# Graph attention kernel: TensorE's block numbers read as one load of ten bytes a group instead of two loads of five words

## The chip, the cores and the metric

The kernel runs on 1 core of one Trainium2 chip. The metric is the device time of one execution in microseconds (us), the median of several runs; lower is better. Engines are named as the profile names them: PE is TensorE (PEld its weight loads), DVE VectorE, ACT ScalarE, POOL GpSimd, SP SyncE. Each engine has a sequencer of its own, written PEq, DVEq and so on, which works through the engine's instruction stream: it waits on semaphores, computes addresses in registers, reads values from memory into registers, and hands matmuls and other work to the engine's queue.

## The reference, cut to what matters

Three graph attention layers over 3125 nodes and 50,000 edges that are sorted by destination, then a mixture of experts. The change lies in the sum over edges of the attention layers:

```
def _gat_layer(x, W, attn_l, attn_r, bias, src, dst, num_heads, head_dim, use_elu):
    z = (x @ W).reshape(N, num_heads, head_dim)
    el = jnp.sum(z * attn_l, axis=-1)
    er = jnp.sum(z * attn_r, axis=-1)
    e = jax.nn.leaky_relu(el[src] + er[dst], NEG_SLOPE)
    m = jax.ops.segment_max(e, dst, num_segments=N)
    ex = jnp.exp(e - m[dst])
    denom = jax.ops.segment_sum(ex, dst, num_segments=N)
    alpha = ex / denom[dst]
    out = jax.ops.segment_sum(alpha[:, :, None] * z[src], dst, num_segments=N)
    ...
x = _gat_layer(node_features, W0, al0, ar0, b0, src, dst, 12, 64, True)
x = _gat_layer(x, W1, al1, ar1, b1, src, dst, 12, 64, True)
x = _gat_layer(x, W2, al2, ar2, b2, src, dst, 1, 768, False)
```

## The kernel before

The program is a chain of stages: a setup, then for each layer `l` a **node sweep** (the product with W, tile by tile of 128 nodes, written to a table in HBM) and an **edge sweep**, then a layer norm with routing, and the experts. In the trace the three edge sweeps stand at 250 to 902, 1107 to 1760 and 1954 to 2608 us.

**An edge sweep** walks over 415 visits. A visit is a tile of 128 edges together with one of 25 blocks of 128 destination nodes. POOL gathers the 128 source rows of a visit by an indirect DMA (L672) into a ring of 20 places, DVE multiplies them by their weights (L1492), and PE adds them up: a one-hot matrix of the visit times the rows, 384 and 396 columns wide, into the accumulator of the visit's block (`add_up`, L1047). Which accumulator it is, and which part of `erp` (the destination side of the attention logits) a visit needs, depends on the block number b(k) of visit k, which is known only at run time. So PE's sequencer must have b(k) in a register before it can issue.

**Groups.** Five visits make a group (G = 5), 83 groups a sweep (NG). Four groups (jj = 0 to 3, NBUF = 4) make one trip of a loop on the device (`pe.Fori`, L1070 in the profile); the last trip, of three groups, stands outside of the loop. The places of a trip are numbered at = jj * 5 + j.

**What PE does for a group**, in the order in which it is written, in `body`: visits j = 0 to 4; behind visit 1 the `er_of_edges` products (three small matmuls of 24 columns each, L1022) of two visits of the group three ahead (ER_LEAD = 3), which is 6 matmuls, and behind visit 3 those of the other three visits, 9 matmuls. DVE and ACT make of them the weights of that group.

**Two forms of visit.** Most visits are two fp32 matmuls, of which the trace has four records (two passes each). The places in SPLIT (2, 7, 10, 12, 17 in the first two layers, 1, 4, 7, 11, 14, 17 in the third) are done as two fp32r parts, `parts`: also four records, but shorter ones. Ahead of either PE's sequencer waits on semaphores of DVE and ACT: for the rows, the one-hot matrix and a free accumulator.

**Block numbers.** The setup on DVE writes b(k) as int32 into `b_k`, and from there copies: `b_of` for PE (83 rows of five, in a pitch of 8 words, and three rows of zeros at the end), `b_g` for ACT (first block of a group and of the next), `turns` for POOL (in the experts). PE's sequencer reads a row of `b_of` by `blocks_of(g)` (L1012), one TENSOR_LOAD of five values with a register instruction (FUSED_REGOPS) for its address ahead of it. In a group there are two: `now`, the group's own row, ahead of visit 0, and `later`, the row of group g + 3, behind visit 0. Ahead of each sweep three more groups have only their `er_of_edges` (45 matmuls), each behind a load.

The edge loop of PE is the only code that the change moves:

```
now = blocks_of(g)
for j in range(G):
    add_up(g, i, jj, j, now[j])
    if j == 0 and ahead:
        later = blocks_of(g + ER_LEAD)
    if j in (1, 3) and ahead:
        for n in ((0, 1), (2, 3, 4))[j // 2]:
            er_of_edges(g + ER_LEAD, (jj + ER_LEAD) % NBUF, n, later[n])
```

Of the kernel before, what the change touches and what calls it, by code (L numbers as in the profile page):

```python
# [8 lines left out]
I32 = mybir.dt.int32  # L9
U32 = mybir.dt.uint32  # L10
U8 = mybir.dt.uint8
# [14 lines left out]
G = 5  # L26
NBUF = 4
IN_ARENA = 3
ER_LEAD = 3
# [3 lines left out]
NG = V // G  # L33
# [14 lines left out]
NS = (TOP * N + EX * (P - 1)) // P  # L48
# [8 lines left out]
class Chain:  # L57
# [5 lines left out]
    def link(self, instruction):  # L63

        self.mark(instruction)
        self.follow()
# [33 lines left out]
def gnn_ffn(nc, x, edges, gnn, ffn, out):  # L100
    with ExitStack() as ctx:
        def sb(name, shape, dt=F32):
            return ctx.enter_context(nc.sbuf_tensor(name, shape, dt))
# [62 lines left out]
        src_k = sb("src_k", [P, V], I32)  # L166
        dst_k = sb("dst_k", [P, V])
        b_k = sb("b_k", [1, V + 1], I32)
        b_g = sb("b_g", [1, NG, 4], I32)
        b_of = sb("b_of", [1, NG + ER_LEAD, 8], I32)  # L170
        ends = sb("ends", [1, NB], I32)
        turns = sb("turns", [1, NS], I32)
        erm = sb("erm", [P, NB, 2 * HMAX])
        ert = sb("ert", [P, NB, HMAX])
        erp = sb("erp", [P, NB * 3 * 2 * HMAX], BF16)
# [247 lines left out]
        def at_place(j, b):  # L423

            return place_first[:, j, b, :] if b < EARLY else place_last[:, j, b - EARLY, :]
# [5 lines left out]
        def numbers():  # L431

            at = 8 * D + TOP * NB * NS
            return arena_h[:, at:at + 2 * TOP * NB * NS].rearrange("p (w j b s) -> p w j b s", w=2, j=TOP, b=NB)
# [494 lines left out]
        def _(pe):  # L929
# [74 lines left out]
            def edge_sweep(l):  # L1004
# [2 lines left out]
                for bank in range(4):  # L1007
                    nc.tensor.matmul(PS[:, bank, :], zeros_h[:, 0:P], zeros_h[:, :], start=True, stop=True)

                def blocks_of(g):  # L1010

                    return nc.values_load_multi_w_load_instructions(  # L1012
                        b_of[0:1, bass.ds(g, 1), 0:G].rearrange("o i j -> o (i j)"), engines=[mybir.EngineType.PE],
                        min_val=0, max_val=NB - 1,
                        skip_runtime_bounds_check_because="b(k) is a sum of NB - 1 comparisons")[1]

                def er_of_edges(g, jj, j, b):

                    if j == 0:
                        pe.wait_ge(s_ST, g + (NG * l + 1))  # L1020
                    for part in range(3):
                        o = nc.tensor.matmul(er_of(l, jj)[:, j, :], ST_b[:, jj, j * P:(j + 1) * P],  # L1022
                                             erp[:, bass.ds(b * (6 * H) + part * 2 * H, 2 * H)],
                                             start=(part == 0), stop=(part == 2))
                    if j == G - 1:
                        o.then_inc(s_er, 1)
# [23 lines left out]

                def body(i, last):
                    groups = LAST_GROUPS if last else NBUF
                    for jj in range(groups):
                        g = NBUF * i + jj
                        ahead = not last or jj + ER_LEAD < groups
                        now = blocks_of(g)
                        for j in range(G):
                            add_up(g, i, jj, j, now[j])
                            if j == 0 and ahead:
                                later = blocks_of(g + ER_LEAD)  # L1060
                            if j in (1, 3) and ahead:
                                for n in ((0, 1), (2, 3, 4))[j // 2]:
                                    er_of_edges(g + ER_LEAD, (jj + ER_LEAD) % NBUF, n, later[n])

                pe.wait_ge(s_erm, l + 1)
                for g in range(ER_LEAD):
                    now = blocks_of(g)
                    for j in range(G):
                        er_of_edges(g, g, j, now[j])
                with pe.Fori(0, NI - 1) as i:  # L1070
                    body(i, False)
                body(NI - 1, True)

            for l in range(3):
                node_sweep(l)
                edge_sweep(l)
# [44 lines left out]
            for j in range(TOP):  # L1121
                pe.wait_ge(s_onehots, j + 1)
                pe.wait_ge(s_numbered, j + 1)
                for b in range(NB):
                    if b == EARLY:
                        pe.wait_ge(s_late_places, j + 1)
                    o = nc.tensor.matmul(PS[:, 6, 0:2 * NS], at_place(j, b), numbers()[:, :, j, b, :],
                                         start=(j == 0 and b == 0), stop=(j == TOP - 1 and b == NB - 1))
# [70 lines left out]
        def _(dve):  # L1199
            dc = Chain(dve, s_dve)  # L1200
            link = dc.link
# [54 lines left out]
            starts = b_k[0:1, 0:V].rearrange("o (g j) -> o g j", j=G)  # L1256
# [1 line left out]
            link(nc.vector.tensor_copy(b_g[0:1, :, 0:1], starts[:, :, 0:1]))  # L1258
            link(nc.vector.tensor_copy(b_g[0:1, 0:NG - 1, 1:2], starts[:, 1:NG, 0:1]))
            link(nc.vector.memset(b_of[0:1, :, :], 0))  # L1260
            link(nc.vector.tensor_copy(b_of[0:1, 0:NG, 0:G], starts))
            link(nc.vector.tensor_copy(ends[0:1, 0:NB - 1], enter[0:1, :]))
            link(nc.vector.memset(ends[0:1, NB - 1:NB], V))
            augment_first((2, 3, 4))
# [595 lines left out]
```

## Time and profile before

| | |
|---|---|
| median of 3 runs | 2812.51 us (2811.25 to 2815.1) |
| span of the profiled execution | 3059.8 us |
| mean granted TensorE clock in it | 0.964 |
| PE, PEld busy | 2691.3, 1838.6 us (88%, 60%) |
| DVE, ACT, POOL busy | 2096.8, 1244.9, 1506.0 us |
| chain that ended last | PE 50%, DVE 21%, issue 13% |

The profiled execution has its own time, the 3059.8 us of its span, which is 247 us (8.8%) more than the median of the runs that were timed. Durations below come from that one execution. PE is busy for most of it, but a busy PE isn't PE at its peak: the end of a matmul is modelled, and a record lasts longer than the time until the next one can start. So times between starts are read, rather than durations, where matmuls stand in a row. What the sequencer does (loads of registers, register arithmetic) counts as idle on the engine's line; it can be seen where one asks for a source line.

### The profile page before, as it was taken

The numbers are of one execution on the slowest core, as the hardware profiler recorded it, in microseconds if no ns is written. First come the engines' busy times: TensorE is split into PE (matmuls) and PEld (weight loads), VectorE is DVE, ScalarE is ACT, GpSimd is POOL, SyncE is SP. The second block draws the span as 40 slices with busy tenths as digits, with TensorE's granted clock in tenths as the row PEclk, the third lists the DMA queues.
The fourth block names the chain that finished last, engine by engine and source line by source line (L and its number), as shares of the span: only waits on it lengthen the run. The fifth ranks groups of instructions, "written<-read, shape, count | busy, mean of one in ns | idle before, by whom it ended". The sixth has DMA issues, their size and how long they took to land.

```text
span 3059.8 us, 57119 instructions
## 1 busy us (share of the span) xinstructions
PE 2691.3 (88%) x14056; PEld 1838.6 (60%) x14060; DVE 2096.8 (69%) x3895; ACT 1244.9 (41%) x2607; POOL 1506.0 (49%) x1528
## 2 busy tenths in 40 slices
PE   3997999998989979898989999788898889759998
PEld 2884555555558855555555578555555555547776
DVE  6776888888887768888878877545555555673332
ACT  1224555555544435555555544223222223622211
POOL 1005666666631156666666412466666665114443
PEclk9998999999999979999999999899999999979999
DMA  6447888888867878888888767788888887967776
GB/s 210 169 148 251 289 286 291 291 290 290 289 219 205 210 228 292 289 287 290 291 287 288 250 191 216 218 281 285 279 282 281 282 282 258 397 217 145 145 146 118
DMA packets 199261, 762.09 MB, mean 249 GB/s; under 512 B 41889, under 2 KB 58033, under 8 KB 198542
## 3 DMA queue, kind: packets, MB, share of 16 engines
q0 software_dynamic: 127632, 604.14, 64.8%
q1 hardware_dynamic: 53790, 108.21, 11.6%
q10 hardware_dynamic: 17760, 48.79, 4.0%
q8 instruction: 36, 0.59, 0.1%
q14 instruction: 43, 0.35, 0.0%
HBM read 640.01 MB, written 133.45 MB: 253 GB/s over the span
## 4 chain that ended last, share of the span: by engine, by line
PE 50%; DVE 21%; issue 13%; ACT 4%; DMA 4%; another core or an unknown queue 3%; SPq 2%; POOL 1%; DVEq 1%; ACTq 1%; POOLq 0%
PE PS L1047 30%; DVE arena L1492 5%; PE PS L1176 5%; PE PS L978 4%; PE PS L1165 4%; PE PS L980 2%; DVE parts L1509 2%; PE PS L1022 2%; DMA arena<-table,src_k 2%; SPq L493 1%; DVE ST_b L1445 1%; DVE arena L1357 1%; DVE arena L1367 1%; DVE arena L1335 1%
## 5 line engine op out<-in xcount | busy, mean ns | idle before, releaser
L672 POOL DMA_INDIRECT arena<-table,src_k x945 | 959.9, 1016 | 500.8 <-issue 213.1
L1047 PE MATMUL PS<-arena,S 128*128 128x384 f32 (+1 forms) x1848 | 706.8, 514 | 57.8 <-issue 46.3
L1492 DVE TENSOR_TENSOR arena<-arena,PS 128x768 f32<-128x768 f32 x630 | 575.2, 946 | 0.9 <-ACT arena L822 0.9
L1047 PEld LDWEIGHTS PS<-arena,S 128*128 128x128 f32 x1848 | 335.5, 194 | 282.7 <-issue 156.8
L1047 PE MATMUL PS<-parts,S 128*128 128x384 f32 (+2 forms) x1332 | 340.4, 375 | 57.2 <-issue 51.0
L672 POOL DMA_INDIRECT W<-table,src_k x300 | 295.9, 986 | 160.5 <-PE PS L1047 71.2
L1047 PE MATMUL PS<-arena,S_weighted 128*128 128x384 f32 (+1 forms) x840 | 319.9, 516 | 33.4 <-issue 25.3
L1022 PEld LDWEIGHTS PS<-erp,ST_b 128*128 128x128 bf16 x3735 | 193.9, 97 | 249.9 <-issue 184.2
L618 POOL DMA_DIRECT2D table<-arena x75 | 41.6, 555 | 557.7 <-DVEq L1379 382.3
L1047 PEld LDWEIGHTS PS<-parts,S 128*128 128x128 f32 x1332 | 223.7, 192 | 106.0 <-issue 97.5
L830 ACT ACTIVATE apart<-iota_row,dst_k 128x128 f32<-128x128 f32 x830 | 261.7, 389 | 60.8 <-issue 44.1
L781 ACT ACTIVATE parts<-arena 128x780 fp32r<-128x780 f32 x168 | 142.0, 849 | 309.2 <-DVE arena L1492 136.7
L1022 PE MATMUL PS<-erp,ST_b 128*128 x3735 | 213.0, 172 | 54.0 <-issue 38.9
L1047 PE MATMUL PS<-W,S 128*128 128x396 f32 (+1 forms) x640 | 239.8, 502 | 14.6 <-issue 8.1
L1047 PEld LDWEIGHTS PS<-arena,S_weighted 128*128 128x128 f32 x840 | 154.3, 196 | 143.7 <-issue 79.4
L978 PE MATMUL PS<-W_lead,S 128*128 128x512 f32 x450 | 190.4, 423 | 9.8 <-DVE xT_rest L1383 7.9
L1509 DVE TENSOR_TENSOR parts<-arena,parts 128x780 fp32r<-128x780 f32 x168 | 162.0, 964 | 35.7 <-issue 24.4
L1492 DVE TENSOR_TENSOR W<-W,PS 128x768 f32<-128x768 f32 x200 | 182.4, 944 | 0.0
L978 PE MATMUL PS<-W_lead,xT_rest 128*128 128x512 f32 x450 | 179.2, 398 | 0.0
L978 PE MATMUL PS<-W_rest_r,S 128*128 128x512 f32 x450 | 178.7, 397 | 0.0
L1047 PEld LDWEIGHTS PS<-W,S 128*128 128x128 f32 x640 | 116.1, 190 | 91.3 <-issue 39.0
L1795 DVE TENSOR_SCALAR arena<-PS,gate_of 128x768 f32<-128x768 f32 x56 | 57.0, 1018 | 162.5 <-PE PS L1176 162.5
(293 smaller groups left out, 4354.1 us busy)
## 6 DMA issues: line engine op xcount, KB each, us to landing
arena<-mixed SPq DMA_DIRECT2D x63, 384.0 KB, 3.6
table<-arena POOLq DMA_DIRECT2D x50, 396.0 KB, 3.3
local_b<-local SPq DMA_DIRECT2D x123, 160.0 KB
mixed<-sums ACTq DMA_DIRECT2D x50, 384.0 KB
arena<-table SPq DMA_DIRECT2D x50, 384.0 KB, 4.6
arena<-table,src_k POOLq DMA_INDIRECT x945
table<-arena POOLq DMA_DIRECT2D x25, 384.5 KB, 4.6
out<-last_bias POOLq DMA_DIRECT2D x25, 384.0 KB, 6.4
```

What stands on the lines that cost most here:

```text
L672: nc.gpsimd.indirect_dma_start(edge_row(l, k % U)[:, 0:table_width(l)], None, table[l][:, :], bass.IndirectOffsetOnAxis(src_k[:, k:k + 1]. ...
L781: nc.scalar.activation(parts[:, n, 0, 0:D + H], row[:, 0:D + H], ACT.Copy).then_inc(s_leading, 1)
L830: o = nc.scalar.activation(apart[:, j, :], iota_row[:, :], ACT.Abs, scale=-1.0, bias=dst_k[:, bass.ds(g * G + j, 1)])
L978: nc.tensor.matmul(PS[:, 4 + 2 * b.q, :], rows[x_part], W_parts[W_part][:, 0:512], start=start, stop=stop)
L980: o = nc.tensor.matmul(PS[:, 5 + 2 * b.q, 0:z_width(l) - 512], rows[x_part], W_parts[W_part][:, 512:z_width(l)], start=start, stop=stop)
L1022: o = nc.tensor.matmul(er_of(l, jj)[:, j, :], ST_b[:, jj, j * P:(j + 1) * P], erp[:, bass.ds(b * (6 * H) + part * 2 * H, 2 * H)], start=(p ...
L1047: o = nc.tensor.matmul(flat[:, bass.ds(odd * 1024 + 512 * c, n)], onehot, row[:, c * HALF:c * HALF + n], start=False, stop=True, skip_grou ...
L1165: o = nc.tensor.matmul(to, token_xT(b.q)[:, k * P:(k + 1) * P], WiT[:, k, bass.ds(e * FF, FF)], start=(k == 0), stop=(k == KC - 1))
L1176: o = nc.tensor.matmul(PS[:, 4 + 2 * b.q + c, 0:HALF], hT(b.q)[0:rows, j * P:(j + 1) * P], flat[0:rows, bass.ds(e * (2 * D) + (2 * c + j) ...
L1492: nc.vector.tensor_tensor(z, z, a, ALU.mult).then_inc(s_msg, 1)
L1509: nc.vector.tensor_tensor(low[:, 0:D + H], row[:, 0:D + H], f32(high[:, 0:D + H]), ALU.subtract).then_inc(s_rest, 1)
L1795: nc.vector.tensor_scalar(zr(b.q, D).rearrange("p (c d) -> p c d", c=2), PS[:, 4 + 2 * b.q:6 + 2 * b.q, 0:HALF], gate_of[:, bass.ds(b.n, 1 ...
```

## The change

PE's two loads a group become one. A row of `b_of` is now ten bytes in a pitch of 16: the five block numbers of group g and the five of group g + 3. `blocks_of(g)` reads ten values by one TENSOR_LOAD (five, by a parameter, ahead of the sweep). The first group of a loop trip loads at its start, as before; each other group's row is loaded in the group before it, behind visit 2. The last group of a trip loads nothing. `b_g` and `turns` become bytes too, so ACT's and POOL's loads of them read bytes. The setup has one more copy on DVE. In all PE has 258 loads (9 of five, 249 of ten) where it had 498.

```
-        b_g = sb("b_g", [1, NG, 4], I32)
-        b_of = sb("b_of", [1, NG + ER_LEAD, 8], I32)
+        b_g = sb("b_g", [1, NG, 4], U8)
+        b_of = sb("b_of", [1, NG, 16], U8)
...
-        turns = sb("turns", [1, NS], I32)
+        turns = sb("turns", [1, NS], U8)
...
-                def blocks_of(g):
+                def blocks_of(g, of_groups=2):
...
-                        b_of[0:1, bass.ds(g, 1), 0:G].rearrange("o i j -> o (i j)"), engines=[mybir.EngineType.PE],
+                        b_of[0:1, bass.ds(g, 1), 0:of_groups * G].rearrange("o i j -> o (i j)"), engines=[mybir.EngineType.PE],
...
                     groups = LAST_GROUPS if last else NBUF
+                    blocks = blocks_of(NBUF * i)
                     for jj in range(groups):
                         g = NBUF * i + jj
                         ahead = not last or jj + ER_LEAD < groups
-                        now = blocks_of(g)
+                        now, later = blocks[:G], blocks[G:]
                         for j in range(G):
                             add_up(g, i, jj, j, now[j])
-                            if j == 0 and ahead:
-                                later = blocks_of(g + ER_LEAD)
+                            if j == 2 and jj + 1 < groups:
+                                blocks = blocks_of(g + 1)
...
                 for g in range(ER_LEAD):
-                    now = blocks_of(g)
+                    now = blocks_of(g, 1)
...
             link(nc.vector.memset(b_of[0:1, :, :], 0))
-            link(nc.vector.tensor_copy(b_of[0:1, 0:NG, 0:G], starts))
+            link(nc.vector.tensor_copy(b_of[0:1, :, 0:G], starts))
+            link(nc.vector.tensor_copy(b_of[0:1, 0:NG - ER_LEAD, G:2 * G], starts[:, ER_LEAD:, :]))
```

How PE's instructions stand, at two places of the first layer. In these rows ISA and REGISTER_ALU at L1035, L1039 and L1042 compute a visit's addresses, ISA at L1047 is the register instruction of a matmul, and `parts` marks a visit in two parts. The first place is the start of the group jj = 2, whose visit 0 is one in two parts. Before:

```order
L1012 ISA
L1012 TENSOR_LOAD b_of
L1035 REGISTER_ALU
L1042 REGISTER_ALU
L1047 ISA
L1047 MATMUL PS<-parts,S 128x384 x2
L1047 ISA
L1047 MATMUL PS<-parts,S 128x396 x2
L1012 ISA
L1012 TENSOR_LOAD b_of
L1039 ISA
L1042 REGISTER_ALU
```

Now:

```order
L1035 REGISTER_ALU
L1042 REGISTER_ALU
L1044 REGISTER_ALU
L1047 ISA
L1047 MATMUL PS<-parts,S 128x384 x2
L1047 ISA
L1047 MATMUL PS<-parts,S 128x396 x2
L1039 ISA
L1042 REGISTER_ALU
```

Both loads are gone from here; visits 0 and 1 follow on each other. The second place is visit 2 of the group jj = 0, also one in two parts (its place is 2). Before, it goes straight on to visit 3:

```order
L1047 MATMUL PS<-parts,S 128x384 x2
L1047 ISA
L1047 MATMUL PS<-parts,S 128x396 x2
L1039 REGISTER_ALU
L1042 REGISTER_ALU
L1047 ISA
```

Now the load of ten stands between the two:

```order
L1047 MATMUL PS<-parts,S 128x384 x2
L1047 ISA
L1047 MATMUL PS<-parts,S 128x396 x2
L1012 ISA
L1012 TENSOR_LOAD b_of
L1039 REGISTER_ALU
L1042 REGISTER_ALU
```

It stands there in the groups jj = 0, 1 and 2 of each trip, and in the first two layers visit 2 of each of these is one in two parts.

## Rows read from the trace of the kernel before

**Rows 1.** Busy time by stretch, the three edge sweeps: length, engines, clock, DMA.
```profile
core 0: us, PE busy (x) PEld busy (x) DVE busy (x) ACT busy (x) POOL busy (x), PEclk, DMA share, GB/s
250.00:902.00 652.00, 588.77 (x2905) 353.15 (x2905) 542.99 (x780) 350.12 (x831) 419.92 (x413) 0.97 0.87 285
1107.00:1760.00 653.00, 580.55 (x2905) 349.79 (x2905) 543.21 (x781) 349.49 (x831) 416.69 (x413) 0.97 0.86 284
1954.00:2608.00 654.00, 576.33 (x2905) 353.65 (x2905) 347.53 (x1091) 184.41 (x406) 413.14 (x415) 0.96 0.86 278
sum 1959.00, PE 1745.65 PEld 1056.59 DVE 1433.73 ACT 884.01 POOL 1249.75; mean PE 581.88 PEld 352.20 DVE 477.91 ACT 294.67 POOL 416.58
```

**Rows 2.** Waits of PE in the whole execution: us in total, times, longest.
```profile
PE PS L1047 <- issue: 136.5, 283, 5.0
PE PS L1022 <- issue: 38.9, 70, 1.3
...
PE PS L1047 <- DVE arena L1492: 15.0, 19, 3.2
PE PS L1022 <- DVE ST_b L1445: 14.0, 3, 6.1
```

**Rows 3.** Sequencers' loads, each source line's own view: duration ns min/median/max.
```profile
L1012 PEldq TENSOR_LOAD <-b_of x498: 5/582/1751, 249.9 to 2596.9; - x166
...
L1155 PEldq TENSOR_LOAD <-expert_at x28: 765/769/783, 2733.8 to 3030.6; - x28
...
L1809 DVEq TENSOR_LOAD <-expert_at x28: 520/524/901, 2739.5 to 3033.5; - x28
...
L790 ACTq TENSOR_LOAD <-b_g x249: 4/494/907, 272.9 to 2601.3; - x125
...
L799 ACTq TENSOR_LOAD <-ends x75: 282/287/378, 299.9 to 2602.3; - x75
...
L641 POOLq TENSOR_LOAD <-turns x53: 283/288/508, 2766.5 to 3044.8; - x53
```

**Rows 4.** Timeline of PE ahead of the first sweep: start, length, work [idle before].
```profile
250.89 1.96 PE L1022 MATMUL PS<-erp,ST_b 128*128 x15 [6.11 <-DVE ST_b L1445]
253.43 2.13 PE L1022 MATMUL PS<-erp,ST_b 128*128 x15 [0.58 <-issue]
256.15 2.02 PE L1022 MATMUL PS<-erp,ST_b 128*128 x15 [0.58 <-issue]
```

**Rows 5.** Timeline of PE in the second sweep, group 2, nothing late.
```profile
1145.50 1.17 PE L1047 MATMUL PS<-parts,S 128*128 128x384 f32 x4
...
1146.51 1.47 PE L1047 MATMUL PS<-arena,S 128*128 128x384 f32 x4
1147.81 0.30 PE L1022 MATMUL PS<-erp,ST_b 128*128 x6
1147.97 0.95 PE L1047 MATMUL PS<-parts,S 128*128 128x384 f32 x4
1148.76 1.47 PE L1047 MATMUL PS<-arena,S 128*128 128x384 f32 x4
1150.07 0.38 PE L1022 MATMUL PS<-erp,ST_b 128*128 x9
```

**Rows 6.** Timeline of PE, visits 0 and 1 of a group jj = 2: first and last.
```profile
315.21 0.98 PE L1047 MATMUL PS<-parts,S 128*128 128x384 f32 x4
316.45 1.57 PE L1047 MATMUL PS<-arena,S 128*128 128x384 f32 x4 [0.26 <-issue]
...
1724.65 1.12 PE L1047 MATMUL PS<-parts,S 128*128 128x384 f32 x4
1725.91 1.57 PE L1047 MATMUL PS<-arena,S 128*128 128x384 f32 x4
```

**Rows 7.** Timeline of PE, other visits behind a load: first and last.
```profile
330.24 0.50 PE L1047 MATMUL PS<-W,S 128*128 128x396 f32 x1
330.90 1.57 PE L1047 MATMUL PS<-arena,S 128*128 128x384 f32 x4 [0.17 <-issue]
...
2578.74 0.33 PE L1022 MATMUL PS<-erp,ST_b 128*128 x6
2579.29 2.85 PE L1047 MATMUL PS<-arena,S_weighted 128*128 128x384 f32 x8 [0.22 <-issue]
```

**Rows 8.** Timeline of POOL: the indirect DMAs of the gathers.
```profile
377.28 0.95 POOL L672 DMA_INDIRECT arena<-table,src_k  x1 [0.30 <-issue]
378.54 1.18 POOL L672 DMA_INDIRECT arena<-table,src_k  x1 [0.30 <-issue]
```

**Rows 9.** DVE's copy into `b_of` in the setup, its line's own view.
```profile
L1261 DVE COPY b_of<-b_k x1: 580/580/580, 25.5 to 25.5; 1x415 int32<-1x415 int32 x1
```

## The prediction

> **What bounds the kernel now.** I read the busy times by stage first [rows 1]. The three edge sweeps take 1959.0 of the 3059.8 us of the profiled execution, and the change touches nothing else of weight. PE is busy for 89% of them, DVE for 83% in the first two and 53% in the third, POOL for 64%, and the DMA engines for 86 to 87%. Next the waits of PE [rows 2]: for DVE it waits 29 us in all, but for "issue", which is time in which no engine held it up, 136.5 us ahead of visits and 38.9 us ahead of the small matmuls. So PE is held by its own array or by its own sequencer.
>
> To tell these two apart I put a group's work side by side. **The array**, from starts in a stretch without a late visit [rows 5]: an fp32 visit takes 1.31 us (1148.76 to 1150.07), one in two parts 0.79 (1147.97 to 1148.76), the small matmuls 0.16 for 6 and 0.23 for 9. A group with one visit in two parts is 4 x 1.31 + 0.79 + 0.39 = 6.42 us; one with two of them is 5.9. **The sequencer**: ahead of the sweep it has only loads and small matmuls, and there it sets the pace [rows 4]. Fifteen of them span 1.96 us, of which the last record is about 0.20, so one costs (1.96 - 0.20) / 14 = 0.126 us; from one group of fifteen to the next are 2.54 us, so 2.54 - 15 x 0.126 = 0.65 for a load, and 0.83 in the other case. The load itself lasts 0.582 us [rows 3]. I take 0.69 with its address instruction. A visit's own issue comes out of the place where a load binds: from visit 0 to visit 1 of a group jj = 2 the starts are 1.24 us apart [rows 6], and 1.24 - 0.69 = 0.55. A group then asks 15 x 0.126 + 2 x 0.69 + 5 x 0.55 = 6.0 us of the sequencer, just below the array's 6.4. The group really takes (652 - 11) / 83 = 7.7 us in the profile, sweep's start left out.
>
> The profile adds much of that. The timed runs are 247 us shorter. If all of this came off the sweeps, a group would take (1959 - 247) / 249 = 6.9 us there, and PE's idle time in them, 1959.0 - 1745.7 = 213 us with some 30 for three starts, would hardly be left. So **there is not much to win**: whatever the loads cost in the timed runs lies between 6.4 and 6.9 us a group, 0.45 x 249 = 112 us in all, with every other cause in it.
>
> **The change part by part. Loads removed.** 498 loads of five become 9 of five and 249 of ten, at 0.69 us of sequencer time each. Where it runs ahead of the array, as in [rows 5], a load costs nothing: the second load of that group lies between 1145.50 and 1146.51, and visit 1 is hardly late. Where it has no lead, a load shows. In the groups jj = 2 of the first two sweeps, visit 0 gives the array 0.79 us of work and the sequencer needs 1.24 for load and visit 1: 0.45 us lost, 16 or 18 times a sweep, 34 in all, of which [rows 6] are the first and the last. I sum their excess over the array's own step to 13.6 us. Behind loads at other places (visit 0 of any group, visit 1, and in the third sweep the visit 2 behind a visit in two parts) I find 85 more gaps of 0.15 to 0.6 us, the first and the last in [rows 7], 29.7 us together. In sum **43 us of the profiled execution** stand behind a load. Longer gaps, up to 5.0 us, I don't count: they also come where no load stands, and the profile must add its 247 us somewhere.
>
> **Loads added and moved.** The price of a load of ten bytes is what no row shows. The nearest rows are [rows 3]: one value 0.287 us, two 0.494 (ACT) and 0.524 (DVE), three 0.769 (PE), and five only 0.582. One to three grow by 0.24 a value; five break the line. Either four neighbours come in one trip, about like one value, and the rest singly (five = a four and a one), or from some size on a load has a fixed price of 0.58. By the second, or if bytes that fill words come as words (ten bytes = three words, 0.77), ten cost **0.58 to 0.77**; by the first, two fours and two ones, **0.58 + 0.24 x 2 and a bit, some 1.1**; if bytes are taken one by one, **0.287 + 9 x 0.241 = 2.46**. The lower end for anything is 0.287. I take 0.6 to 0.8, because the five-value row on this very engine is the nearest.
>
> The group's sequencer time becomes 1.9 + 2.75 + 0.11 + load: 5.3 to 5.5 us at 0.58 to 0.77, 5.9 at 1.1, 7.2 at 2.46, against 6.0 before.
>
> **Its new place.** Behind visit 2 the load stands ahead of visit 3, and waiting behind it are visit 3 and the 9 small matmuls, from which DVE makes the weights of three groups on. In sweeps 1 and 2 visit 2 has two parts in all the groups where it stands, so the array has 0.79 us there and the sequencer needs 0.69 + 0.55 = 1.24: the same 0.45 us that cost time in the groups jj = 2, now in three groups of four. But the lead is another. Before, two loads stood ahead of this point in the group (1.4 us); now none in jj = 1 and 2 and one in jj = 0. Two fp32 visits gain the sequencer 2 x (1.31 - 0.55) = 1.5 us, and six small matmuls take 0.76 - 0.16 = 0.6 of it, so it comes to visit 2 with some 0.9 us in hand, twice the 0.45. Visit 0 of jj = 0 keeps its load and its gap (7.6 of the 43 us). I put back 7.6 for that and 12 for places where the lead isn't there: 43 - 7.6 - 12 = **23 us gained**.
>
> **The rest.** One more copy on DVE in the setup, 0.6 us or less by the one that stands beside it [rows 9], at 25 us of a stretch in which PE waits for it at most once: up to 0.6 us. ACT's and POOL's loads of bytes (249 of two, 53 of one) lie on engines that are half idle in these stages (ACT 884 of 1959 us); nothing there is on PE's path, and I take 0, with 249 x 0.2 us hidden either way.
>
> **The sum.** 3059.8 - 23 + 0.6 = 3037 for the profiled execution, and 2812.5 - 23 + 0.6 = **2790 us** for the median. That the whole 43 us exist outside of the profile isn't sure; if half do, the gain is 12.
>
> **A rule that speaks against it.** The row of five shows 0.582 us, 0.116 a value [rows 3]. The Trainium skill, Runtime: NRT & Kernel Launch, Instruction fetch mechanics, says that a TENSOR_LOAD costs about 200 ns a register even in bulk, measured on loads from HBM. By that five would be 1.0 and ten 2.0 us (an estimate by the page), the same work in one lump. The trace disagrees for five, while one to three values come near it. By contrast the page DMA: Bandwidth & Descriptors, Latency and other measured facts, gives a load a floor of about 600 ns, which the rows of one value (0.287) contradict.
>
> **The rivals.** (a) **Ten bytes cost about 1.1 us.** For it: the step of 0.24 a value in three rows, and five as four and one. The sequencer gains 6.0 - 5.9 = 0.1 us a group, the two bad places go, but behind visit 2 it needs 1.1 + 0.11 + 0.55 = 1.76 us against 0.79 of work and a lead of 0.9, so it is late there now and then. Gain 0 to 18 us, 2803. (b) **Slower: the bytes come one by one**, at 2.46 us. The sequencer then needs 7.2 us a group against the 6.9 of today: at least 0.3 x 249 = 75 us; and since it comes in one lump (2.57 + 0.55 = 3.1 us against 0.79 of work and a lead that the queue limits), up to 1.0 us a group, 250 us. 2890 to 3060, taken as 2950. It decides from about 1.6 us, where the lump exceeds work and lead. For it: one to three values at 0.24 each, and that a byte is a smaller unit than a word. Against it: the row of five. (By the rule of the runtime page above, 2.0 us, the outcome would be on this side too.) (c) **Covered anyway.** In the timed runs the sequencer keeps its lead, or others are next: POOL starts a gather every 1.26 us [rows 8], 6.3 us a group, and the DMA engines at a share of 0.87 and 7.7 us a group would be full at 6.7. Then a faster sequencer moves nothing: 2807 to 2816, 2812. (d) A price between 1.3 and 1.9 us: 2815 to 2860.
>
> **How the numbers follow.** My case 40%, 2788 with its own range of 2765 to 2806. (a) 25%, (c) 10%, (b) 20%, (d) 5%. The range leaves out (b) and reaches to the rest: 2762 to 2860. A measurement of this kernel tells 0.2%, 5.6 us, from no change. Faster by more: 0.36 of mine, 0.15 of (a), 0.01 of (c), 0.52. Within: 0.03, 0.09, 0.08, 0.01, 0.21. Slower: 0.01, 0.01, 0.01, 0.20 of (b), 0.04 of (d), 0.27.
>
> **What would show it.** L1012 in the profile of the changed kernel has 258 loads, and their median says at once which case it is: 0.6 to 0.8, 1.1, or above 2. In the groups jj = 2 the starts of visits 0 and 1 stand 0.8 to 1.0 us apart instead of 1.24, and "issue" ahead of L1047 falls from 136.5 us towards 115. Wrong for the time even at a cheap load: new gaps ahead of visit 3, or waits for DVE, gathers or POOL in the place of "issue". If the load is cheap, the gaps are gone and the time is the same, it is (c).

## The result, and the profile after

The changed kernel takes 2987.55 us, median of 4 runs (2983.6 to 2992.33); the kernel before, in the same comparison, 2811.88 (2806.32 to 2815.1, 4 runs). The ratio is 1.0621, with a 95% interval of 1.0601 to 1.0640: **176 us slower**, where 22 us faster was forecast. The profiled execution took 2987.78 us, its span 2986.2.

The row that the prediction had asked for says at once which case it is. The sequencers' loads of the changed kernel, each from its source line's own view, as in [rows 3]; one for PE, ACT, POOL, and PE again:

```profile
L1012 PEldq TENSOR_LOAD <-b_of x258: 1222/2394/3802, 249.4 to 2520.0; - x129
```

```profile
L790 ACTq TENSOR_LOAD <-b_g x249: 467/474/856, 272.0 to 2525.3; - x125
```

```profile
L641 POOLq TENSOR_LOAD <-turns x53: 271/275/495, 2692.4 to 2971.2; - x53
```

```profile
L1156 PEldq TENSOR_LOAD <-expert_at x28: 765/770/787, 2659.4 to 2957.0; - x28
```

A load of ten bytes takes 2.39 us; the five bytes of the nine loads ahead of the sweeps take 1.22 (the least value of the row). The loads that stayed small cost what they did: two values 0.474 where words took 0.494, one value 0.275.

The three edge sweeps, in the columns of [rows 1]:

```profile
250.00:882.00 632.00, 560.59 (x2906) 343.59 (x2907) 544.49 (x783) 349.58 (x833) 416.54 (x413) 0.98 0.88 293
1084.00:1724.00 640.00, 565.28 (x2905) 345.27 (x2905) 544.53 (x782) 348.59 (x832) 416.02 (x412) 0.97 0.87 290
1916.00:2532.00 616.00, 544.34 (x2905) 339.55 (x2905) 345.69 (x1090) 184.15 (x406) 414.04 (x415) 0.98 0.88 295
sum 1888.00, PE 1670.20 PEld 1028.41 DVE 1434.71 ACT 882.32 POOL 1246.60; mean PE 556.73 PEld 342.80 DVE 478.24 ACT 294.11 POOL 415.53
```

This is less than the 1959.0 of [rows 1], though the kernel is slower. The trace of before comes from an execution of 3060 us, not of 2812. The last part of the experiments shows what is different in that trace, and why the two can't be subtracted.

The waits of PE (us in total, times, longest), as in [rows 2]:

```profile
PE PS L1047 <- issue: 114.7, 142, 3.1
PE PS L1047 <- DVE arena L1494: 54.1, 58, 1.9
...
PE PS L1022 <- DVE ST_b L1447: 15.5, 3, 6.7
...
PE PS L1047 <- DVE S_weighted L1500: 13.1, 11, 2.2
```

"Issue" ahead of visits fell from 136.5 to 114.7 us, just the number that the prediction had named for a gain. It proves nothing: the 136.5 come from the trace of 3060 us, and part of the time went under DVE's name, 15.0 to 54.1 us. The timeline of the first sweep shows what that name is worth (start, length, engine and work; PEld is the weight load). This is one trip, visits 2 and 3 of the groups jj = 0, 1 and 2:

```profile
299.16 1.80 DVE L1494 TENSOR_TENSOR arena<-arena,PS 128x768 f32<-128x768 f32 x2
...
301.79 0.94 PEld L1047 LDWEIGHTS PS<-arena,S 128*128 128x128 f32 x4 [1.48 <-issue]
```

```profile
299.69 0.95 PE L1047 MATMUL PS<-parts,S 128*128 128x384 f32 x4
301.79 1.57 PE L1047 MATMUL PS<-arena,S 128*128 128x384 f32 x4 [1.16 <-DVE arena L1494]
...
307.65 0.96 PE L1047 MATMUL PS<-parts,S 128*128 128x384 f32 x4
308.97 1.57 PE L1047 MATMUL PS<-arena,S 128*128 128x384 f32 x4 [0.36 <-issue]
...
311.73 1.18 PE L1047 MATMUL PS<-parts,S 128*128 128x384 f32 x4
312.75 1.47 PE L1047 MATMUL PS<-arena,S 128*128 128x384 f32 x4
...
314.21 0.96 PE L1047 MATMUL PS<-parts,S 128*128 128x384 f32 x4
316.12 1.57 PE L1047 MATMUL PS<-arena,S 128*128 128x384 f32 x4 [0.95 <-DVE W L1494]
```

DVE had been done at 300.96, 0.83 us before the visit at 301.79 that is said to have waited for it; the weight load of the same visit, which starts with it, is put down to "issue" rather. From visit 2 to visit 3 are 2.10, 1.32 and 1.91 us, where the two parts give the array 0.79. So the three gaps are 1.31, 0.53 and 1.12 us, and ahead of each stands a load. "Late" is the time from the start of one visit to the start of the next, beyond what the array needs for the visit and the small matmuls between. Summed over all starts in the trace, visit 3 is late by 61.3, 64.1 and 61.4 us in the three sweeps: **187 us, 1.0 us for each of the 186 loads that stand there**. (Such sums leave small excesses out; with every one counted, those of this document come out 6 to 22 us higher.) In the first two sweeps the median is 1.24 us in jj = 0, 0.53 in jj = 1 and 1.15 in jj = 2. The load of jj = 0 follows soon on the one at the trip's start, and jj = 2 has its visit 0 in two parts; jj = 1 has only fp32 visits since the last load, and there the sequencer gets a lead. The loads at a trip's start aren't free either: the 60 that stand behind a visit 4 make visit 0 late by 52 us, 0.87 each. The pair at 311.73 is visits 0 and 1 of jj = 2, now 1.02 us apart instead of 1.24 [rows 6]: that part of the change works.

### The profile page after: what moved, and what is told of

The parts are those of the page before. It is cut to its first block, busy times and chain, and to the rows that moved or that the text cites. A ratio compares the mean times of both kernels' runs of the same rounds, so it can differ in the third digit from the quotient of the medians.

```text
span 2986.2 us, 56700 instructions
## 1 busy us (share of the span) xinstructions
PE 2616.9 (88%) x14056; PEld 1809.5 (61%) x14060; DVE 2093.3 (70%) x3896; ACT 1240.9 (42%) x2607; POOL 1504.2 (50%) x1528
## 4 chain that ended last, share of the span: by engine, by line
PE 49%; DVE 19%; issue 11%; DMA 8%; ACT 5%; POOL 4%; SPq 2%; ACTq 1%; DVEq 1%; POOLq 0%
PE PS L1047 29%; DMA arena<-table,src_k 6%; DVE arena L1494 5%; PE PS L1177 5%; PE PS L978 5%; PE PS L1166 4%; POOL arena L672 3%; PE PS L980 3%; DVE parts L1511 2%; DVE W L1494 2%; PE PS L1022 2%; SPq L493 1%; DVE arena L1337 1%; DVE arena L1358 1%; DVE arena L1359 1%
## 5 line engine op out<-in xcount | busy, mean ns | idle before, releaser
L1047 PE MATMUL PS<-arena,S 128*128 128x384 f32 (+1 forms) x1848 | 704.3, 516 | 137.4 <-issue 72.1
L1047 PEld LDWEIGHTS PS<-arena,S 128*128 128x128 f32 x1848 | 334.4, 193 | 366.8 <-issue 211.3
L1047 PE MATMUL PS<-arena,S_weighted 128*128 128x384 f32 (+1 forms) x840 | 317.8, 509 | 67.9 <-issue 42.6
L1047 PE MATMUL PS<-parts,S 128*128 128x384 f32 (+2 forms) x1332 | 340.3, 377 | 0.8 <-DVE parts L1511 0.8
L1022 PEld LDWEIGHTS PS<-erp,ST_b 128*128 128x128 bf16 x3735 | 172.4, 97 | 204.3 <-issue 141.3
L1047 PEld LDWEIGHTS PS<-arena,S_weighted 128*128 128x128 f32 x840 | 149.6, 192 | 181.1 <-issue 114.5
L1047 PEld LDWEIGHTS PS<-parts,S 128*128 128x128 f32 x1332 | 224.9, 189 | 27.2 <-issue 1.6
L1047 PE MATMUL PS<-W,S 128*128 128x396 f32 (+1 forms) x640 | 232.5, 496 | 0.0
L1022 PE MATMUL PS<-erp,ST_b 128*128 x3735 | 180.1, 171 | 23.0 <-DVE ST_b L1447 15.5
L650 POOL DMA_INDIRECT out<-arena,target_of x56 | 89.0, 1590 | 160.1 <-DMA out<-arena,target_of 129.9
```

Of the source, the lines that this page charges most:

```text
L650: nc.gpsimd.indirect_dma_start(out[:, :], bass.IndirectOffsetOnAxis(target_of[:, n:n + 1].bitcast(U32), 0), zr(n % 2, D), None, compute_op ...
L1047: o = nc.tensor.matmul(flat[:, bass.ds(odd * 1024 + 512 * c, n)], onehot, row[:, c * HALF:c * HALF + n], start=False, stop=True, skip_grou ...
```

## Experiments

The chip of the first comparison took 2812 us for the kernel before. The comparisons below ran on five chips, on which it took 2809, 3038, 3064, 3066 and 3036 us; each run is compared with the runs of before on its own chip.

**What a load costs.** The changed kernel with 48 loads more on PE in the setup, each of its values used by one small matmul; nothing else is changed.

```diff
+            pe.wait_ge(s_probe, 3)
+            def probe(kind, at, n):
+                values = nc.values_load_multi_w_load_instructions(kind[0:1, at:at + n], ...)[1]
+                for v in values:
+                    nc.tensor.matmul(PS[:, 7, 0:24], zeros_h[:, 0:P], zeros_h[:, bass.ds(v, 24)], start=True, stop=True)
+            for turn in range(2):
+                for kind, sizes in ((probe_w, (1, 2, 3, 4, 5, 6, 8, 10, 12, 16)), (probe_h, (1, 4, 5, 8, 10)), (probe_b, (1, 2, 4, 5, 8, 10))):
+                    for n in sizes:
+                        probe(kind, 0, n)
+                for at, n in ((1, 4), (2, 4), (3, 5)):
+                    probe(probe_w, at, n)
```

> The changed kernel with 48 loads of zeros more on PE's sequencer in the setup, in two rounds: 1, 2, 3, 4, 5, 6, 8, 10, 12 and 16 words, 1, 4, 5, 8 and 10 halfwords, 1, 2, 4, 5, 8 and 10 bytes, and 4, 4 and 5 words from the words 1, 2 and 3 of a row. The changed kernel's ten-byte load took 2.394 us, 0.24 a byte. Theory 'words come in fours': 4 words cost about as much as 1 or little more (0.29 to 0.34 us), 5 words 0.58, 8 words about 0.6 to 0.65, 10 words 1.1, 12 words 0.9 to 1.0; bytes and halfwords 0.24 each, whatever their number. Rival 'a fixed price from some size on': 4 or 5 to 16 words all about 0.58. If alignment to 16 bytes is what makes a four, the loads from word 1 and 2 cost 0.24 a value, some 1.0 us.

Some loads of the first round, each from the view of its line in a window that holds it alone (duration ns; `probe_w` are words, `probe_h` halfwords, `probe_b` bytes). Four, eight, ten and twelve words, four words from the second on, one, five and ten bytes:

```profile
L944 PEldq TENSOR_LOAD <-probe_w x1: 338/338/338, 6.6 to 6.6; - x1
```

```profile
L944 PEldq TENSOR_LOAD <-probe_w x1: 599/599/599, 10.3 to 10.3; - x1
```

```profile
L944 PEldq TENSOR_LOAD <-probe_w x1: 1078/1078/1078, 12.0 to 12.0; - x1
```

```profile
L944 PEldq TENSOR_LOAD <-probe_w x1: 856/856/856, 14.3 to 14.3; - x1
```

```profile
L944 PEldq TENSOR_LOAD <-probe_w x1: 1014/1014/1014, 41.5 to 41.5; - x1
```

```profile
L944 PEldq TENSOR_LOAD <-probe_b x1: 300/300/300, 30.3 to 30.3; - x1
```

```profile
L944 PEldq TENSOR_LOAD <-probe_b x1: 1222/1222/1222, 33.1 to 33.1; - x1
```

```profile
L944 PEldq TENSOR_LOAD <-probe_b x1: 2384/2384/2384, 37.9 to 37.9; - x1
```

All of them (ns, second round; it differs from the first by less than 20 ns but for one and three words):

| values | 1 | 2 | 3 | 4 | 5 | 6 | 8 | 10 | 12 | 16 |
|---|---|---|---|---|---|---|---|---|---|---|
| words | 310 | 553 | 765 | 337 | 607 | 826 | 597 | 1075 | 854 | 1112 |
| halfwords | 301 | | | 997 | 1217 | | 1917 | 2387 | | |
| bytes | 303 | 534 | | 985 | 1221 | | 1917 | 2386 | | |

Four words that begin at a multiple of four come together, for about 0.26 us a four; every other value costs about 0.24 by itself. Bytes and halfwords come together in none of the counts tried, up to ten, and neither do four words from the second or third on (1.01 us). Where the load begins decides: five words from the fourth on hold a whole aligned four, and yet they take 1.24 us, five times the single price. That is why five words cost 0.58 [rows 3], a four and a one, and why ten words (two fours and two ones) cost more than twelve.

**What the element type does to the kernel, and what the plan does.** Three kernels on the chip of 2809 us. In the first only the small arrays are bytes (`b_g` and `turns`), PE's loads are two of five words in their old places, and each block number is masked, because the next kernel needs it:

```diff
-        b_g = sb("b_g", [1, NG, 4], I32)
+        b_g = sb("b_g", [1, NG, 4], U8)
-        turns = sb("turns", [1, NS], I32)
+        turns = sb("turns", [1, NS], U8)
+                    b = b & 31
```

> The kernel before with `b_g` and `turns` in bytes, and with each visit's block number masked by & 31 in a register instruction of its own (needed, as the wait against a loaded word must not be negative). The base for the runs with words. One more register instruction of 0.09 us a visit is 0.45 us of sequencer time a group (6.0 becomes 6.5 us, against 6.4 for the array). If the sequencer bounds the timed runs as well, up to 249 x 0.3 = 75 us slower (2890); if it has slack there, 2812 to 2830.

2830.47 us, ratio 1.0088 (1.0062 to 1.0114): 21 us, which is 17 ns for each of the 1245 masks, if they are all of it. Its trace is the nearest there is to the kernel before on such a chip, and PE's "issue" ahead of visits is 23.6 us in it, against 136.5 in [rows 2]:

```profile
PE PS L1048 <- issue: 23.6, 80, 0.4
```

The second is the changed kernel, its ten values in words:

```diff
+                    b = b & 31
-        b_of = sb("b_of", [1, NG, 16], U8)
+        b_of = sb("b_of", [1, NG, 12], I32)
```

> The changed kernel with `b_of` in words again (one load of ten words a group, at the changed kernel's place), masked as e0. Theory 'price': the load falls from 2.39 to about 1.1 us and nearly all of the 176 us come back: 2810 to 2850, at or a little below e0. Rival 'place': the lump behind visit 2 is what costs, and it stays well slower than e0, by 50 us or more.

2817.84 us, ratio 1.0035 (1.0018 to 1.0052). The third is the kernel before, its two loads of five in their old places, in bytes:

```diff
-        b_of = sb("b_of", [1, NG + ER_LEAD, 8], I32)
+        b_of = sb("b_of", [1, NG + ER_LEAD, 8], U8)
```

> The kernel before with all three tables in bytes and nothing moved: two loads of five bytes a group, at the places of before. By the price each costs 1.22 us instead of 0.58 (five-byte loads of the changed kernel), 2.45 a group, as much as the one load of ten. Theory 'price': as slow as the changed kernel, 2950 to 3000. Rival 'place or lump': two shorter loads between visits hide better, 2830 to 2900, and then the place had its part in the loss.

3022.27 us, ratio 1.0760 (1.0736 to 1.0784), above both forecasts. The PE loads of the three, then the first sweep of the first kernel, its three sweeps summed, and the sum of the third's:

```profile
L1012 PEldq TENSOR_LOAD <-b_of x498: 577/583/1605, 252.1 to 2357.9; - x166
```

```profile
L1012 PEldq TENSOR_LOAD <-b_of x258: 581/1082/2453, 250.5 to 2351.9; - x129
```

```profile
L1012 PEldq TENSOR_LOAD <-b_of x498: 1216/1222/2627, 251.4 to 2557.6; - x166
```

```profile
251.00:826.00 575.00, 551.62 (x2903) 337.23 (x2904) 538.62 (x780) 349.06 (x831) 430.28 (x414) 0.98 0.92 323
sum 1720.00, PE 1641.99 PEld 1003.40 DVE 1430.24 ACT 882.60 POOL 1265.97; mean PE 547.33 PEld 334.47 DVE 476.75 ACT 294.20 POOL 421.99
```

```profile
sum 1922.00, PE 1714.21 PEld 1000.42 DVE 1435.22 ACT 882.21 POOL 1245.36; mean PE 571.40 PEld 333.48 DVE 478.41 ACT 294.07 POOL 415.12
```

The type alone costs 3022.27 - 2809.0 = **213 us**, more than the whole change. Merging and moving the loads brings time in both types: 2830.47 - 2817.84 = 12.6 us in words (the intervals of the two ratios don't overlap), and in bytes 35 to 39 (3022.27 to 2987.55 us, or ratio 1.0760 to the change's 1.0621, from two comparisons with a kernel before of 2809 and 2812 us). Against the kernel before itself the ten words are 0.35% slower, since they need the masks. With bytes in the old places the lateness sits behind the old places: summed over the starts, visit 1 is late by 168 us, visit 0 by 80, against some 26 and 25 in the first kernel. With ten words visit 3 is late by 46 us in all, with ten bytes by 187. So it isn't the merging and mostly not the place: it is what bytes cost, 2.39 us in one load or 1.22 in each of two.

**Can cheaper loads win?** If time follows the loads, loads in aligned fours should beat both. In the first of four more kernels PE reads a trip's block numbers straight from `b_k` in loads of 8, 8, 4, 8 and 8 words, each value used by its own group and by the group three ahead of it; 312 loads in all.

```diff
-                    blocks = blocks_of(NBUF * i)
+                    read(0, 8)
...
+                            if (jj, j) == (0, 0):
+                                read(12, 8)
+                            if (jj, j) == (0, 3):
+                                read(8, 4)
+                            if (jj, j) == (1, 0) and not last:
+                                read(20, 8)
+                            if (jj, j) == (1, 4) and not last:
+                                read(28, 8)
```

> The masked base (e0) with other loads: a trip of four groups needs 35 neighbouring block numbers, and they are read straight from `b_k` in words, in loads of 8, 8, 4, 8 and 8 that all start at a multiple of four. By the measured prices (0.60, 0.60, 0.34, 0.60, 0.60, and 0.11 for each address) that is 3.3 us a trip, where e0 has 8 x (0.58 + 0.11) = 5.5 and the kernel of ten words 4 x (1.08 + 0.11) = 4.8. Theory 'price' (sequencer time is what counts, at part of its length): 0.55 us a group less than e0, of which a third to two thirds shows: 45 to 90 us would be all of it, 15 to 50 expected, so 2780 to 2815. Rival 'covered by now': at 6.3 to 6.4 us a group the array or POOL (one gather every 1.26 us) bounds, and it is no better than the ten words: 2810 to 2825.

The second has, instead of a masked block number at each visit, one wait on `s_acc_free` a group, for the block of its last visit:

```diff
-                    pe.wait_ge(s_acc_free, b + (NB * l + 1))
+                    if j == 0:
+                        pe.wait_ge(s_acc_free, (last_b & 31) + (NB * l + 1))
```

> e5 with one wait for a free accumulator a group (for the block of its last visit) instead of one a visit, and the mask once: four masks and four sums less in a group, 0.35 to 0.75 us of sequencer time. If the sequencer still bounds, another 10 to 40 us less than e5; if array, POOL and DMA are reached, the same as e5 within 5 us. In all 2765 to 2805.

The third is e0, the masked kernel with two loads of five words, with this one wait; the fourth is the ten-word kernel reading twelve:

```diff
-                        b_of[0:1, bass.ds(g, 1), 0:of_groups * G].rearrange("o i j -> o (i j)"), engines=[mybir.EngineType.PE],
+                        b_of[0:1, bass.ds(g, 1), 0:12 if of_groups == 2 else G].rearrange("o i j -> o (i j)"), engines=[mybir.EngineType.PE],
```

Of the third:

> e0 (two loads of five words) with the one wait a group alone. Sequencer time 6.5 minus 0.35 to 0.75 us a group. The sum of what e5 and this one gain over e0 (2830) against e6 tells whether they come out of the same budget: if the sequencer bounds throughout they add up; if something else is reached, e6 is less than the sum. Expected 2795 to 2815.

Of the fourth:

> The kernel of ten words with two more words read and not used: 12 aligned words cost 0.855 us in the table of prices, 10 cost 1.078. Theory 'words come in fours': reading more is cheaper, 0.22 us a group on the sequencer, so 0 to 30 us less than the ten words (2818): 2795 to 2818. If the count of values set the price it would be slower by up to 249 x 0.24 x 2 = 120 us.

The chip took 3037.55 us for the kernel before. Ratios: loads in fours 1.0032 (1.0020 to 1.0044), with one wait 0.9988 (0.9979 to 0.9997), two loads of five with one wait 1.0000 (0.9990 to 1.0009), twelve words 1.0031 (1.0019 to 1.0044). Nothing moves by more than 0.32%. The one comparison with like masks and like waits is the second kernel against the third: by the prices its loads are 0.55 us a group cheaper, 137 us in all, and it takes 3033.52 against 3036.15 us, 0.1% less, with intervals that overlap. So here the time doesn't follow the price of the loads. For the first and the fourth, their bases (e0 and the ten words) weren't run on this kind of chip, so their masks stand against the cheaper loads, and what twelve words do against ten stays open. I ran three of them again on another chip, and with them the changed kernel with its load at the start of the load's own group:

```diff
-                    blocks = blocks_of(NBUF * i)
...
+                        blocks = blocks_of(g)
...
-                            if j == 2 and jj + 1 < groups:
-                                blocks = blocks_of(g + 1)
```

Of the loads in fours:

> e5 once more. Its first runs stood beside a kernel before of 3037.6 us, as in the first profile of before (3059.8), while the changed kernel and e0 to e3 stood beside one of 2809 to 2812. In the traces of 3040 to 3060 us register instructions of PE and ACT stretch to some 700 ns (187 of PE in the profile of before, 253 in e5's); in the traces of the others there is none. On a chip without these the price theory expects e5 at 2780 to 2815 (e0 2830), the rival 'covered' 2825 to 2840. If this call meets such a chip again, both stay within 0.5% of before.

Of the fours with one wait:

> e6 once more, for the same reason. On a chip as that of the changed kernel's runs: 2765 to 2805, faster than before by 0.2 to 1.5%, if sequencer time still shows; equal to before within 0.2% if array, POOL or DMA are reached.

Of the twelve words:

> e9 once more. Twelve aligned words against ten: at or below the ten words' 2818 (ratio to before 1.0035), 2795 to 2818 by 'words come in fours'; above it by 30 us and more if the count set the price.

Of the ten bytes at the group's own start:

> The changed kernel (ten bytes in one load, 2.39 us) with the load at the start of its own group, ahead of visit 0, for every group, instead of a group early behind visit 2. The sequencer's sum is the same, 7.15 us a group. Theory 'price alone': as slow as the changed kernel within 15 us (ratio to before 1.057 to 1.067). Rival 'place has a part': ahead of it stands visit 4 with 1.31 us of array work instead of a visit in two parts with 0.79, so up to 0.5 us in three groups of four is hidden: 50 to 75 us faster than the changed kernel (ratio 1.035 to 1.045).

Again a chip of the slower kind, 3064.33 us for before: 1.0031 (1.0019 to 1.0043), 0.9981 (0.9972 to 0.9990), 1.0040 (1.0024 to 1.0055), and the ten bytes at the group's own start 1.0095 (1.0073 to 1.0118). The last one is the surprise: a load of 2.39 us in each group, and one per cent, not six. So I ran the changed kernel itself again, with three of these beside it; it met a chip of the same kind.

> The changed kernel once more, beside the others of this call. If the kernel before takes 2803 to 2817 here, 2975 to 3000 as at first. If it takes 3030 to 3070, as it did for e5 to e10, the long load and the 0.7 us stretches of the sequencer compete: theory 'the stretches are a store that runs dry (they come only where the sequencer issues faster than it is fed)' says the long loads are hidden in them, and it stays within 2% of before, 3060 to 3120; rival 'they add up': 6% over before, 3210 to 3250.

Of the ten bytes at the group's start, of the fours, and of the fours with one wait:

> Ten bytes in one load at the group's start, beside the changed kernel with the same load a group early behind visit 2. 'Price alone': equal within 15 us. 'Place has a part': e10 is 50 to 75 us faster where before takes 2810.

> Aligned fours straight from b_k, masked in each visit. Where before takes 2810: 2780 to 2815 by price, 2825 to 2840 if covered. Where it takes 3030 to 3070: 0.3% above before, as twice before.

> The same with one wait a group. Where before takes 2810: 2765 to 2805. Where it takes 3030 to 3070: 0.1 to 0.2% below before, as twice before.

On this chip before takes 3065.62 us, and **the changed kernel 3094.81, ratio 1.0102** (1.0085 to 1.0118): 29 us slower, not 176. The load at the group's start: 3111.23, 1.0136 (1.0108 to 1.0165); the fours 1.0024 (1.0010 to 1.0038), with one wait 0.9979 (0.9969 to 0.9988). Two of them once more:

> The changed kernel with the ten-byte load at its own group's start for every group. On a chip where the kernel before takes about 2810 us: if the place behind visit 2 adds cost of its own (my step on the new place), this is below the changed kernel's 2988 by 10 us or more; if the early place helps (the load finds the lead of three visits), above it, some 3000 to 3020. On a chip where the kernel before takes 3040 to 3065, again 1.010 to 1.014 of it.

> Block numbers of 35 neighbours a trip in aligned loads of 4 and 8 words, one acc_free wait and one mask a group. On a chip where the kernel before takes 3040 to 3065, again 0.998. On one where it takes about 2810: if loads and register work of PE's sequencer bind there too, 2795 to 2808 (0.995 to 0.999); if the masks cost more than the cheaper loads save, 2812 to 2825 (1.001 to 1.005).

On one more chip, of 3036.14 us, they have 1.0121 (1.0100 to 1.0141) and 0.9984 (0.9974 to 0.9994), about as on the others. A chip of 2810 us, on which these two would have told more, wasn't met again.

**Where the two kinds of chip differ.** Register instructions of PE's sequencer, from the views of the matmuls' line and of the addresses' line (duration ns, min/median/max). First the changed kernel on the first chip, then the same kernel on the chip of 3066 us, then the kernel before as profiled, with the addresses' line of the first and the last:

```profile
L1047 PEldq FUSED_REGOPS  x2490: 46/72/114, 262.4 to 2526.1; - x192
```

```profile
L1047 PEldq FUSED_REGOPS  x2490: 2/46/729, 263.3 to 2626.4; - x192
```

```profile
L1047 PEldq FUSED_REGOPS  x2490: 2/51/1412, 261.2 to 2602.2; - x192
```

```profile
L1042 PEldq ALU_OP  x1245: 32/32/36, 262.1 to 2525.4; - x178
```

```profile
L1042 PEldq ALU_OP  x1245: 2/32/737, 260.9 to 2601.5; - x178
```

In the five traces from chips of the quick kind no such instruction of PE takes more than 0.114 us. In the others some take 0.70 us and a few 1.4, and some next to them 2 ns. Counted from the records, in the trace of before 188 of them last 0.6 to 1.5 us, 133 us together, and 58 on ACT; there are none on DVE and POOL. All traces from chips on which before takes 3036 us or more have them, none from those on which it takes 2809 to 2812. Each of the five chips was met in one comparison only, so whether the chip itself makes the difference or something else that all runs of a comparison share isn't separated; "kind of chip" stands for either. One of them stands ahead of a small matmul in the trace of before:

```profile
L1022 PEldq FUSED_REGOPS  x1: 701/701/701, 303.3 to 303.3; - x1
```

In the changed kernel on the chip of 3066 us there are only 84 of them, 60 us together. It isn't this trace alone: the four traces of kernels with loads of ten bytes have 84 to 96, the eleven others of this kind 112 to 264. So the long loads and the stretches don't add up, they partly take each other's place. The sweeps there, same columns as above:

```profile
sum 1984.00, PE 1695.57 PEld 1041.01 DVE 1432.01 ACT 884.07 POOL 1237.89; mean PE 565.19 PEld 347.00 DVE 477.34 ACT 294.69 POOL 412.63
```

Of its 1984 us visit 3 is late by 215, about as on the first chip; but on this kind the kernel before starts from 1959 [rows 1], where on the quick kind a kernel with loads of five words needs some 1720. Not all of these 239 us are accounted for: even counted up to the sequencer's next instruction, the 188 stretches make 178 us. The stretches crowd at a few places of the four-group trip (in the last run of the fours, 33 of 130 stand between the visits 3 and 4 of jj = 0), which would fit instructions that arrive late. That is argued, not shown; what stretches them stays open.

## Why the prediction was wrong

- **The price of the load is the step that failed.** "I take 0.6 to 0.8, because the five-value row on this very engine is the nearest": it measured 2.39. The bound of 2.46 was right, and so was its reading, one value after another at 0.24. The row of five was nearest in size but not in kind: it holds words from a multiple of four on, and the change makes them bytes. I had weighed "five = a four and a one" and gave it 1.1 us for ten; that is what ten words take (1.08). I carried it over to bytes, for which no row spoke.
- **Rival (b) is what happened**, at a chance of 20% and outside the range. Its price, 2890 to 3060 taken as 2950, holds 2988. It asked up to 1.0 us a group of the lump; 186 loads at 1.0 us make 187 us, on a lead of 2.41 + 0.04 + 0.55 - 1.79 = 1.2 us where I had 0.9. That it decides from some 1.6 us on was not tried; at 1.08 us (the ten words) the change gains 12.6 us on its masked base.
- **The rule that spoke against the change.** Ten bytes took 2.39 us, 0.24 a value. The Trainium skill, Runtime: NRT & Kernel Launch, Instruction fetch mechanics, has about 200 ns a register even in bulk, for loads from HBM; by that an estimate of 2.0 us, and the outcome on the right side. The trace agrees for bytes and not for aligned words (eight in 0.60). The floor of about 600 ns, from the Trainium skill, DMA: Bandwidth & Descriptors, Latency and other measured facts, doesn't hold here: one value takes 0.275 to 0.31.
- **"The profile adds 247 us" was wrong.** In the kernels profiled afterwards the span is within 2 us of the time of the same execution (2986.2 and 2987.78, 2822.5 and 2824.12, 3084.2 and 3085.8). The trace of before has the marks of the slower kind of chip: 3059.8 us, and 188 stretched register instructions. So the 43 us that stand behind a load in it, and its waits for "issue", were partly read from stretches; the masked kernel on the quick kind has 23.6 us of "issue" ahead of all its visits. The group time that I took in its place, 6.9 us, was near: with two loads of five words the sweep bodies of 562.6, 566.5 and 551.4 us make 6.75 a group.
- **The gain of the plan was sized twice too high**, as far as words can tell: 23 us against 12.6, near the 12 that the prediction gives "if half do". The two aren't quite the same case, for ten words take 1.08 us where the prediction had 0.6 to 0.8. Jj = 2 behaves as said (1.02 us between visits 0 and 1).
- **The new place** isn't what costs: at the group's own start the same load is no better (3111 us against 3095 on one chip, 1.0136 against 1.0102, intervals that overlap), on the slower kind of chip. On the quick kind the whole kernel wasn't tried so, but in the trace of the change a load at a trip's start costs 0.87 us and one behind visit 2 1.0. Rival (c) was right in part. Its number falls: the DMA engines, which I had full at 6.7 us a group, stand at 0.92 of the sweeps with groups of 6.75, and on the quick kind the ten words gain 12.6 us. But on the slower kind loads that are cheaper by 137 us in all bring 0.1%, which the intervals don't tell from nothing.
- **The rest** held: the second copy in the setup takes 0.36 us, and ACT's loads of two bytes and POOL's of one cost what words did.

No version beats the kernel before by more than some 0.2%: the best, loads in fours with one wait a group, has 0.9988, 0.9981, 0.9979 and 0.9984 on four chips of the slower kind.

## What to carry to other kernels

Before a sequencer's load is merged or its array narrowed, look for a row with the same element type and the same alignment, not with the nearest count: here packing words to bytes doubled a load of five and cost more than everything else. Keep such arrays in words, start each load at a multiple of four and read whole fours; but once they are in words, cheaper loads brought this kernel next to nothing. And where a profile's span and the timed runs differ, don't put it down to the profiler: look whether single cheap instructions are stretched, and compare kernels on one chip only.

## What the runs showed of the hardware

Two things that I had not expected. A PE sequencer's load costs 0.34, 0.60, 0.86 and 1.11 us for 4, 8, 12 and 16 aligned words, but 0.99, 1.92 and 2.39 for 4, 8 and 10 bytes or halfwords, so fewer bytes are dearer. And the chip that a comparison lands on matters: the same kernel takes 2809 to 2812 us in two comparisons and 3036 to 3066 in four others, at nearly the same granted clock (0.97 and 0.96), with PE's and ACT's register instructions at times stretched to 0.70 us; a change that costs 6.2% on the one costs 1.0% on the other.
